# Two mixture-of-experts stages of a fused decoder: which engine does the elementwise work, and what TensorE does while the tokens are routed

## The chip, the cores and the metric

One core of one Trainium2 chip. The metric is the device time of one launch in microseconds, the median of three runs. The whole program is one kernel: twelve stages in a fixed order, each a block of instruction streams for the engines TensorE (PE), VectorE (DVE), ScalarE (ACT), GpSimd (POOL) and SyncE (SP), joined by semaphores. Between two stages all engines meet.

## The reference

The reference is a decoder with four layers; each has attention, cross attention and a feed-forward part, and after each `x = layernorm(x + part(x))`. x has 8 batches of 256 tokens, 256 wide, all float32. The change touches the feed-forward parts of layers 0 and 1:

```python
def _moe_forward(x, router_w, w1, w2, shared_gate_up, shared_down, shared_gate_w):   # layer 0: E = 8, K = 2, F = 256
    logits = xf @ router_w
    probs = softmax(logits)
    topw, topi = top_k(probs, K)
    combine = zeros((n, E)).at[arange(n)[:, None], topi].add(topw)
    h = silu(einsum('nd,edf->nef', xf, w1))
    ye = einsum('nef,efd->ned', h, w2)
    routed = einsum('ne,ned->nd', combine, ye)
    gu = xf @ shared_gate_up
    gate, up = (gu[:, :F], gu[:, F:])
    shared = silu(gate) * up @ shared_down
    shared = sigmoid(xf @ shared_gate_w) * shared
    return routed + shared

def _L1_ffn_ref(x, expert_sel, keys, values, route_scale):                           # layer 1: 16 experts of 64, K = 4
    sel_val, sel_index = the four largest of sigmoid(x @ expert_sel), divided by their sum, times route_scale
    scores_all = relu(einsum('btd,edh->bteh', x, keys))
    values_all = einsum('bteh,ehv->btev', scores_all, values)
    out = sum over the four chosen experts of sel_val * values_all
```

## The kernel before, in words

`moe_silu` (stage 2, from L2621) has three stretches.

The front. TensorE makes the logits of all 2048 tokens; VectorE takes the softmax and the two best experts of each, counts the tokens of each expert with two TensorE products (`counted`), and works out a place for each of the 4096 choices in 39 tiles of 128 rows, no tile with two experts. Four `at_place` products by VectorE and `to_table` on TensorE turn that into a table; `rows_known` says that the lists `holds` (which row a slot reads) and `dest` (where its result goes) are there. Meanwhile the shared expert is worked out for `EARLY` = 5 of the 8 batches: `sh_gate` and `sh_up` (8 matmul instructions each) on TensorE, Silu and a copy of the up half on ScalarE, their product on GpSimd (`sh_prod`, L3115), `sh_out` on TensorE, scaled on ScalarE, added to x_nat by GpSimd (`sh_add`, L3122). There is one buffer each of gate, up, product and scaled result.

The tiles. For tile t GpSimd issues an indirect DMA that gathers its rows into one of `XB` = 8 buffers (`gather`, L3127), and one that scatters the tile's result `ye` to the DRAM tensor `planes` (L3147): plane 0 for first choices, plane 1 for second. Its queue is 8 gathers, the add of batch 4, then gather t+8 and scatter t in turn. TensorE, in iteration i, transposes the rows of tile i (`rows_in`), multiplies tile i-1 by w1 (`hidden`), transposes tile i-2 (`hidden_turned`) and multiplies tile i-3 by w2 (`product`). ScalarE copies the turned rows out of the T bank and takes Silu out of the R bank; VectorE copies the turned hidden rows and `ye`, which has `YB` = 4 buffers. T, R and O banks alternate by t % 2.

The tail. When all scatters have landed SyncE reads the planes back in 8 DMAs (quarter q has batches 2q and 2q+1, both planes in one semaphore). TensorE, VectorE and ScalarE work out the shared expert for batches 5 to 7. `summed(q)` on VectorE, `weighed(q)` on ScalarE and `joined(q)` on GpSimd together form x + w0 plane0 + w1 plane1; VectorE takes the statistics, GpSimd the root (`root`), ScalarE normalises (`normed`), TensorE transposes and ScalarE copies to x_t (`turned`).

`moe_relu` (stage 5, from L3175) computes all 16 experts densely. A batch has four groups g of hidden rows (`hidden`, 8 matmul instructions, into one of four R banks), a `spread` that lays the token weights out over the hidden rows (4 matmuls into both T banks, copied to `gates` by ScalarE, twice a batch), `clipped` on VectorE (max with 0, times `gates`, from R to `hid`) and `outputs` (32 instructions). Iteration i of its loop does spread and hidden of batch i, outputs of i-1 and `transposed` of i-2. While VectorE routes, TensorE does the hidden groups of batch 0 and then 22 warming instructions (`keep_warm`, L212), whose results nobody reads.

## Time and profile before

| what | value |
|---|---|
| median of 3 runs | 3213.68 us (3212.23 to 3215.28) |
| the profiled execution | 3215.56 us, of it 3213.8 us span |
| mean granted TensorE clock | 0.97 |
| silu mixture | 988.6 to 1182.2 us |
| relu mixture, routing and loop | 1958.6 to about 2112 us |

"Idle before, releaser" says how long an engine stood idle before an instruction and what ended that; "issue" is time in which nothing that the profile shows was waited for. A granted clock of 1.0 is 2.4 GHz, 0.5 is 1.2 GHz. A fp32 matmul of the code is two instructions in the trace.

### The profile page before, as it was taken

The page shows a single profiled execution, that of the slowest core. Times are in us where ns is not written, and L with a number is a line of the kernel's source. Part 1 is how long each engine was busy: PE and PEld are TensorE (multiplying, and loading weights), DVE is VectorE, ACT ScalarE, POOL GpSimd, SP SyncE. Part 2 cuts the span into 40 slices and gives each one's busy share as a digit, 9 for nine tenths or more (in the row PEclk, how much of TensorE's full clock was granted, in tenths as well). Part 3 has the DMA queues.
Part 4 walks back from the last instruction along what each step waited for, and adds up shares of the span by engine and source line. Part 5 has one row for each costly group of instructions (what it writes and reads, how often), then busy time and mean ns, then how long its engine had stood idle before and what let it go on. Part 6 is the DMA issues. An engine that isn't in the chain of part 4 may idle for free. (4 is left out here: it accounts for less than half of the span.)

```text
span 3213.8 us, 55170 instructions
## 1 busy us (share of the span) xinstructions
PE 2937.8 (91%) x22706; PEld 1864.2 (58%) x22706; DVE 1674.5 (52%) x3021; ACT 1232.3 (38%) x2685; POOL 395.8 (12%) x602
## 2 busy tenths in 40 slices
PE   6999899999998968799999998989989899989898
PEld 3565556666655746556666656856656433336576
DVE  4666444444444344444444443324547799985532
ACT  1333255454442333145444441113323476643111
POOL 1111100000003720000000000000111100000222
PEclk9999999999999979899999999989999999999899
DMA  2001000000011331000000000010000100000242
GB/s 111 17 15 66 9 1 1 1 1 1 1 63 58 98 108 47 9 1 1 1 1 1 1 34 17 1 32 19 17 24 14 46 1 1 1 11 23 96 147 74
DMA packets 40623, 93.81 MB, mean 29 GB/s; under 512 B 4632, under 2 KB 32518, under 8 KB 36792
## 3 DMA queue, kind: packets, MB, share of 16 engines
q1 hardware_dynamic: 34583, 76.70, 6.8%
q0 software_dynamic: 5792, 13.59, 1.4%
q8 instruction: 183, 3.00, 0.4%
q14 instruction: 65, 0.52, 0.1%
HBM read 61.69 MB, written 14.03 MB: 24 GB/s over the span
## 5 line engine op out<-in xcount | busy, mean ns | idle before, releaser
L2337 ACT ACTIVATE prob<-R,neg_max 128x333 f32<-128x333 f32 x512 | 268.6, 538 | 182.4 <-DVE neg_max L2407 182.4
L3893 DVE TENSOR_TENSOR_SCAN arena<-arena,u 128x512 f32<-128x512 f32 x256 | 289.5, 1200 | 0.1
L2407 DVE TENSOR_REDUCE neg_max<-R 128x2 f32<-128x666 f32 x256 | 205.5, 844 | 97.1 <-PE R L2217 97.1
L2413 DVE COPY prob_t<-T 128x384 f32<-128x384 f32 x256 | 141.6, 553 | 188.6 <-PE T L2228 184.2
L2228 PEld LDWEIGHTS T<-const,prob 128*128 128x128 f32 (+1 forms) x1536 | 183.3, 143 | 96.3 <-issue 66.2
L2228 PE MATMUL T<-const,prob 128*128 128x128 f32 (+1 forms) x1536 | 210.0, 273 | 19.7 <-DVE prob_t L2413 19.5
L2344 ACT ACTIVATE prob_t<-T 128x384 f32<-128x384 f32 x256 | 126.1, 493 | 213.4 <-PE T L2228 206.7
L3824 ACT ACTIVATE arena<-delta,neg_a 128x510 f32<-128x510 f32 x256 | 175.6, 714 | 43.7 <-DVE arena L3893 42.9
L2177 PE MATMUL O<-arena,keys_in 128*128 128x512 f32 (+1 forms) x384 | 183.8, 603 | 5.0 <-ACT arena L2318 2.4
L2520 POOL COPY rec_rows<-rec 128x256 f32<-128x256 f32 x128 | 51.2, 400 | 1000.2 <-DVE rec L2418 1000.2
L2172 PE MATMUL O<-keys_in,arena 128*128 128x333 f32 x512 | 170.3, 458 | 1.2 <-DVE arena L2388 1.2
L3727 PE MATMUL R<-arena,diag 64*64 64x512 f32 x1024 | 135.8, 620 | 24.3 <-DVE arena L3893 24.2
L2166 PE MATMUL O<-keys_in,arena 128*128 128x256 f32 x512 | 124.5, 387 | 3.2 <-ACT keys_in L2312 2.4
L2424 DVE TENSOR_TENSOR attn_t<-O,arena 128x256 f32<-128x256 f32 x128 | 53.8, 420 | 131.4 <-ACT arena L2349 131.4
L2188 PE MATMUL O<-arena,attn_t 128*128 128x256 f32 x512 | 117.4, 382 | 1.0 <-DVE ysb L2390 1.0
L2172 PEld LDWEIGHTS O<-keys_in,arena 128*128 128x128 f32 x512 | 88.1, 190 | 40.9 <-DVE arena L2388 7.4
L944 DVE TENSOR_REDUCE neg_max<-R 128x8 f32<-128x2048 f32 (+1 forms) x24 | 55.0, 2292 | 100.0 <-PE R L721 100.0
L2166 PEld LDWEIGHTS O<-keys_in,arena 128*128 128x128 f32 x512 | 92.2, 189 | 22.0 <-ACT q_t L2315 4.2
L2188 PEld LDWEIGHTS O<-arena,attn_t 128*128 128x128 f32 x512 | 94.9, 190 | 15.7 <-DVE ysb L2390 1.8
L2337 ACT ACTIVATION_READ_ACCUMULATOR prob<-R,neg_max 128x1 f32 x512 | 103.9, 203 | 0.0
L2243 PE MATMUL O<-prob_t,v 128*64 128x256 f32 (+1 forms) x768 | 99.2, 394 | 1.3 <-DVE prob_t L2413 1.3
L2177 PEld LDWEIGHTS O<-arena,keys_in 128*128 128x128 f32 (+1 forms) x384 | 60.2, 176 | 69.4 <-issue 51.5
(579 smaller groups left out, 5510.8 us busy)
## 6 DMA issues: line engine op xcount, KB each, us to landing
w<-w_dram SPq DMA_DIRECT2D x16, 1024.0 KB, 6.9
arena<-pack_dram SPq DMA_DIRECT2D x2, 4100.0 KB, 15.0
q_pad<-q_pad SPq DMA_DIRECT2D x24, 224.0 KB, 2.7
arena<-pack_dram SPq DMA_DIRECT2D x4, 1284.0 KB, 6.2
arena<-pack_dram SPq DMA_DIRECT2D x1, 4896.0 KB, 15.1
slots_in<-x_nat SPq DMA_DIRECT2D x2, 2048.0 KB, 8.2
arena<-planes SPq DMA_DIRECT2D x8, 512.0 KB, 7.5
arena<-k_nat SPq DMA_DIRECT2D x16, 224.0 KB, 2.7
```

The lines of the kernel that those rows point to most:

```text
L2166: last = nc.tensor.matmul(bank[:, h * T:(h + 1) * T], wq[:, c, (2 * i + h) * P:(2 * i + h + 1) * P], keys[:, c, CTX:XK], start=(c == 0), s ...
L2172: last = nc.tensor.matmul(bank[:, 0:XK], wkv[:, c, i * P:(i + 1) * P], keys[:, c, :], start=(c == 0), stop=(c == C - 1))
L2177: last = nc.tensor.matmul(bank[0:n, :], keys[:, c, first:first + n], wkv[:, c, XI + i % 2 * BANK:XI + (i % 2 + 1) * BANK], start=(c == 0), ...
L2188: last = nc.tensor.matmul(bank[:, 0:D], attn_t[:, b % 2, c, i * P:(i + 1) * P], wo[:, c, :], start=(c == 0), stop=(c == HP - 1))
L2228: last = nc.tensor.transpose(S.T[0:n, i, kc * P:(kc + 1) * P], prob[:, g % 2, i, first:first + n], S.ident)
L2337: last = nc.scalar.activation(prob[:, g % 2, i, :], S.R[:, g % 2, i * BANK:i * BANK + XK], ACT.Exp, bias=neg_max[:, g % 2, i:i + 1], accum ...
L2344: nc.scalar.activation(prob_t[:, m % 2, 1, :, qt * P:(qt + 1) * P], S.T[:, 1, 0:3 * P].rearrange("p (c q) -> p c q", c=3), ACT.Copy).then_ ...
L2407: nc.vector.tensor_reduce(neg_max[:, g % 2, :], S.R[:, g % 2, :].rearrange("p (i n) -> p i n", i=2)[:, :, 0:XK], AX.X, ALU.max, negate=Tru ...
L2413: nc.vector.tensor_copy(prob_t[:, m % 2, 0, :, qt * P:(qt + 1) * P], S.T[:, 0, 0:3 * P].rearrange("p (c q) -> p c q", c=3)).then_inc(M.pt_ ...
L3727: last = nc.tensor.matmul(sums(i, a)[to:to + HB, :], diag[rows, i % CT, n + a, :], state[rows, (q + a) % HELD, :], start=(a == 1 and n == ...
L3824: nc.scalar.activation(decay[:, q % DEEP, :].rearrange("p (b t) -> p b t", b=PAIR)[:, :, 1:T], delta[:, i % 2, :].rearrange("p (b t) -> p ...
L3893: nc.vector.tensor_tensor_scan(state[:, q % HELD, :], decay[:, q % DEEP, :], u[:, i % 2, :], 0.0, ALU.mult, ALU.add)\
```

## The change

In the silu mixture GpSimd keeps the gathers, the scatters and the small root steps; `sh_prod`, `sh_add` and `joined` leave it. VectorE multiplies gate by up straight from the R bank and adds the scaled result; gate and product buffers are double; `scaled` and 16 `weight` matrices (the identity times each token's second weight, made by ScalarE in the tiles) lie in the unused end of the other weight image. On TensorE the counts come ahead of sh_out(0), sh_out(3) and sh_gate(4) stand ahead of the last two table groups, and the batches 5 and 6 of the shared expert are worked out between the tiles at fixed iterations; for that the tiles use one T and one R bank, and `ye` has 6 buffers. The expert numbers are worked out after `rows_known`. In the tail, TensorE sums x and the weighted second plane in eight PSUM banks (`residual`, `second_choices`), VectorE adds the weighted first plane in one step a token tile (`sums`), and turning starts by batch.

In the relu mixture nine groups (batches 0 and 1, and group 0 of batch 2) are multiplied during the routing, clipped into `hid` (three buffers now) by ScalarE, and weighted by VectorE in place once the gates are there; groups 1 to 3 of batch 2 follow the first spread, and the 22 warming instructions go. One DRAM tensor, `context_values`, is declared and not used.

```diff
-    XB, YB = 8, 4
+    XB, YB = 8, 6
...
+    GATE_AT, UP_AT, OUT_AT = {8: 5, 20: 6}, {11: 5, 23: 6}, {15: 5, 27: 6}
...
+    spare, used = S.arena[(k + 1) % 2], sum(n for _, n in PACK[k + 1].values())
+    scaled = spare[:, used:used + NT * D].rearrange("p (t d) -> p t d", t=NT)
+    weight = spare[:, used + NT * D:used + NT * (D + P)].rearrange("p (t n) -> p t n", t=NT)
...
+        sg = sb("sg", [P, 2, FC * T])
+        prod = sb("prod", [P, 2, FC * T])
...
+        banks = [S.O[:, 0, :], S.O[:, 1, :], S.R[:, 0, 0:BANK], S.R[:, 0, BANK:], S.T[:, 0, :], S.R[:, 1, 0:BANK], S.R[:, 1, BANK:], S.T[:, 1, :]]
         block = ctx.enter_context(nc.Block())
+
+        def shared_bank(b, up):
+            return S.R[:, b % 2 if b < EARLY else 1, up * BANK:(up + 1) * BANK]
 
...
+                    sp.dma_start(plane[:, j, 4 * q:4 * q + 4, :], rows.rearrange("(t p) d -> p t d", p=P))\
+                        .then_inc(second_in[q] if j else first_in[q], 16)
...
             sh_up(1)
-            sh_out(0)
             pe.wait_ge(G.picked, 1)
             pe.wait_ge(S.o_free[0], 1)
             flat = pick[:].rearrange("p j t e -> p (j t e)")
             nc.tensor.matmul(S.O[:, 0, 0:J * E], ones, flat, start=True, stop=True)
             nc.tensor.matmul(S.O[:, 1, 0:J * E], tri, flat, start=True, stop=True).then_inc(G.counted, 1)
-            sh_gate(2)
-            sh_up(2)
+            sh_out(0)
             sh_out(1)
-            sh_gate(3)
-            sh_up(3)
+            for b in (2, 3):
+                sh_gate(b)
+                sh_up(b)
             sh_out(2)
             to_table(0)
             to_table(1)
+            sh_out(3)
             sh_gate(4)
             to_table(2)
             to_table(3).then_inc(G.tabled, 1)
             sh_up(4)
-            sh_out(3)
             sh_out(4)
 
...
-                if t >= 2:
-                    pe.wait_ge(G.xt_sb, t - 1)
-                elif t == 1:
-                    pe.wait_ge(G.sh_scaled, EARLY)
+                if t >= 1:
+                    pe.wait_ge(G.xt_sb, t)
                 for c in range(C):
-                    last = nc.tensor.transpose(S.T[:, t % 2, c * P:(c + 1) * P], xe[:, t % XB, c * P:(c + 1) * P], S.ident)
+                    last = nc.tensor.transpose(S.T[:, 0, c * P:(c + 1) * P], xe[:, t % XB, c * P:(c + 1) * P], S.ident)
...
-                if t >= 2:
-                    pe.wait_ge(G.hid_sb, t - 1)
-                else:
-                    pe.wait_ge(G.sh_gate_sb if t == 0 else G.sh_up_sb, EARLY)
+                pe.wait_ge(G.hid_sb if t else G.sh_gate_sb, t or EARLY)
                 for c in range(C):
-                    last = nc.tensor.matmul(S.R[:, t % 2, 0:D], xe_t[:, t % 2, c, :], W[:, bass.ds(w + (w1_at + c * D), D)],
+                    last = nc.tensor.matmul(S.R[:, 0, 0:D], xe_t[:, t % 2, c, :], W[:, bass.ds(w + (w1_at + c * D), D)],
...
+                if i in GATE_AT:
+                    sh_gate(GATE_AT[i])
+                if i in UP_AT:
+                    sh_up(UP_AT[i])
+                if i in OUT_AT:
+                    sh_out(OUT_AT[i])
...
+            def residual(b):
+                pe.wait_ge(G.sh_added, b + 1)
+                nc.tensor.matmul(banks[b], S.ident, S.x_nat[:, b * TT:(b + 1) * TT, :].rearrange("p t d -> p (t d)"),
+                                 start=True, stop=False, skip_group_check=True)
+
+            def second_choices(q):
+                pe.wait_ge(second_in[q], 16)
+                for tt in range(4 * q, 4 * q + 4):
+                    last = nc.tensor.matmul(banks[tt // TT][:, tt % TT * D:(tt % TT + 1) * D], weight[:, tt, :], plane[:, 1, tt, :],
+                                            start=False, stop=True, skip_group_check=True)
+                last.then_inc(G.summed, 1)
...
+            def turned(b):
+                pe.wait_ge(G.normed, b + 1)
...
+            sh_gate(B - 1)
+            sh_up(B - 1)
+            pe.wait_ge(G.weights_made, NT)
+            for b in range(4):
+                residual(b)
+            sh_out(B - 1)
+            second_choices(0)
+            residual(4)
+            pe.wait_ge(G.sh_gate_sb, B)
+            residual(5)
+            second_choices(1)
+            residual(6)
+            second_choices(2)
+            turned(0)
+            turned(1)
+            residual(7)
+            second_choices(3)
+            for b in range(2, B):
+                turned(b)
...
+                if b >= 2:
+                    act.wait_ge(G.sh_prod, b - 1)
+                nc.scalar.activation(sg[:, b % 2, :], shared_bank(b, 0), ACT.Silu).then_inc(G.sh_gate_sb, 1)
...
-            for b in range(1, EARLY):
-                sh_gate(b)
...
-            sh_out(EARLY - 1)
+            sh_gate(1)
+            act.wait_ge(G.picked, 1)
+            sh_out(0)
+            sh_out(1)
+            sh_gate(2)
+            sh_gate(3)
+            sh_out(2)
+            sh_out(3)
+            sh_gate(4)
+            sh_out(4)
...
+                if i in GATE_AT:
+                    sh_gate(GATE_AT[i])
+                if i in OUT_AT:
+                    sh_out(OUT_AT[i])
+                if i < NT:
+                    nc.scalar.activation(weight[:, i, :], S.ident, ACT.Copy, scale=top[:, i, 1:2]).then_inc(G.weights_made, 1)
...
+            sh_gate(B - 1)
+            sh_out(B - 1)
...
+                    if tt % TT == TT - 1:
+                        last.then_inc(G.normed, 1)
...
+            def sh_prod(b):
+                dve.wait_ge(G.sh_gate_sb, b + 1)
+                dve.wait_ge(G.sh_up_full, b + 1)
+                if b >= 2:
+                    dve.wait_ge(G.sh_out_full, b - 1)
+                nc.vector.tensor_tensor(prod[:, b % 2, :], sg[:, b % 2, :], shared_bank(b, 1), ALU.mult).then_inc(G.sh_prod, 1)
+
+            def sh_add(b):
+                dve.wait_ge(G.sh_scaled, b + 1)
+                x = S.x_nat[:, b * TT:(b + 1) * TT, :]
+                nc.vector.tensor_tensor(x, x, scaled[:, b * TT:(b + 1) * TT, :], ALU.add).then_inc(G.sh_added, 1)
+
+            sh_prod(0)
+            sh_prod(1)
             dve.wait_ge(G.counted, 1)
             nc.vector.tensor_copy(count[:], S.O[:, 0, 0:J * E].rearrange("p (c e) -> p e c", c=J))
...
             for i in range(4):
+                if i % 2 == 0:
+                    sh_prod(2 + i // 2)
                 some = slice(i * J // 4, (i + 1) * J // 4)
...
             nc.vector.tensor_scalar(holds[:], second[:], -1.0, 0.0, ALU.add, ALU.max)
             dve.drain().then_inc(G.rows_known, 1)
+            sh_prod(4)
+            nc.vector.tensor_tensor(behind[:], steps[:, 0:NS].unsqueeze(2).to_broadcast([P, NS, E]),
...
+            nc.vector.tensor_copy(expert_at[:], expert_f[:])
+            dve.drain().then_inc(G.experts_known, 1)
+            dve.wait_ge(G.x_rows, 16)
...
+                if i + 2 in UP_AT:
+                    sh_prod(UP_AT[i + 2])
+                if 2 <= i < 2 + EARLY:
+                    sh_add(i - 2)
+                if i in OUT_AT:
+                    sh_add(OUT_AT[i])
...
-                dve.wait_ge(plane_in[q], 32)
-                for tt in (4 * q, 4 * q + 1):
-                    nc.vector.scalar_tensor_tensor(plane[:, 1, tt, :], plane[:, 1, tt, :], top[:, tt, 1:2], S.x_nat[:, tt, :], ALU.mult, ALU.add)
-                dve.wait_ge(G.joined, q + 1)
-                for tt in (4 * q + 2, 4 * q + 3):
-                    nc.vector.scalar_tensor_tensor(plane[:, 0, tt, :], plane[:, 0, tt, :], top[:, tt, 0:1], S.x_nat[:, tt, :], ALU.mult, ALU.add)
-                dve.drain()
-                for tt in (4 * q, 4 * q + 1):
-                    nc.vector.scalar_tensor_tensor(plane[:, 0, tt, :], plane[:, 0, tt, :], top[:, tt, 0:1], plane[:, 1, tt, :], ALU.mult, ALU.add)
+            def sums(q):
+                dve.wait_ge(first_in[q], 16)
+                dve.wait_ge(G.summed, q + 1)
+                for tt in range(4 * q, 4 * q + 4):
+                    nc.vector.scalar_tensor_tensor(plane[:, 0, tt, :], plane[:, 0, tt, :], top[:, tt, 0:1],
+                                                   banks[tt // TT][:, tt % TT * D:(tt % TT + 1) * D], ALU.mult, ALU.add)
                 dve.drain()
...
-            sh_prod(0)
-            sh_prod(1)
             pool.wait_ge(G.x_rows, 16)
-            sh_add(0)
-            for b in range(2, EARLY):
-                sh_prod(b)
-                sh_add(b - 1)
             pool.wait_ge(G.rows_known, 1)
             for t in range(XB):
                 gather(t)
-            sh_add(EARLY - 1)
...
-            joined(0)
-            joined(1)
-            root(0)
-            joined(2)
-            root(1)
-            joined(3)
-            root(2)
-            root(3)
+            for q in range(4):
+                root(q)
...
+    RAW = 2 * G + 1
...
+        hid = sb("hid", [P, 3, HC, T])
...
+                n = G * (b - 1) + g + 1
                 if b >= 1:
-                    pe.wait_ge(M.exp_done, G * (b - 1) + g + 1)
+                    pe.wait_ge(M.raw_sb if n <= RAW else M.exp_done, n)
...
-            for g in range(1, G):
-                hidden(0, g)
-            keep_warm(nc, S, S.T[:, 1, :], 11)
+            for n in range(1, RAW):
+                hidden(n // G, n % G)
...
-                        if i >= 1:
+                        if i >= 1 and G * i + g >= RAW and i != RAW // G:
...
+                if i == 0:
+                    for n in range(RAW, G * (RAW // G + 1)):
+                        hidden(n // G, n % G)
...
+            for n in range(RAW):
+                act.wait_ge(M.s_full, n + 1)
+                b, g = n // G, n % G
+                nc.scalar.activation(hid[:, b, 2 * g:2 * g + 2, :].rearrange("p c t -> p (c t)"), hidden_bank(g), ACT.Relu).then_inc(M.raw_sb, 1)
...
+                if G * b + g < RAW:
+                    dve.wait_ge(M.raw_sb, G * b + g + 1)
+                    dve.wait_ge(M.kg_ready, 2 * b + g // 2 + 1)
+                    nc.vector.tensor_tensor(some, some, gates[:, g // 2, g % 2, :], ALU.mult).then_inc(M.exp_done, 1)
+                    return
...
+                nc.vector.scalar_tensor_tensor(some, hidden_bank(g), 0.0, gates[:, g // 2, g % 2, :], ALU.max, ALU.mult).then_inc(M.exp_done, 1)
```

## Rows read from the trace of the kernel before

**Rows 1.** The page, part 1: busy time, share of span and instructions of each engine.
```profile
PE 2937.8 (91%) x22706; PEld 1864.2 (58%) x22706; DVE 1674.5 (52%) x3021; ACT 1232.3 (38%) x2685; POOL 395.8 (12%) x602
```

**Rows 2.** Timeline, GpSimd: start, duration, engine, line, operation, count [idle before, releaser].
```profile
1030.33 1.22 POOL L3128 DMA_INDIRECT xe<-slots_in,holds  x1 [0.18 <-issue]
...
1039.39 0.94 POOL L3128 DMA_INDIRECT xe<-slots_in,holds  x1 [0.30 <-issue]
...
1041.80 0.97 POOL L3128 DMA_INDIRECT xe<-slots_in,holds  x1 [0.17 <-issue]
...
1131.90 0.98 POOL L3147 DMA_INDIRECT planes<-ye,dest  x1 [0.30 <-issue]
```

**Rows 3.** Timeline, tiles 0, 6 and 7: first result copied, rows transposed.
```profile
1039.86 0.42 DVE L3061 COPY ye<-O 128x256 f32<-128x256 f32 x1 [0.44 <-PE O L2816]
...
1043.99 0.38 PE L2789 MATMUL T<-const,xe 128*128 128x128 f32 x2
...
1046.16 0.38 PE L2789 MATMUL T<-const,xe 128*128 128x128 f32 x2
```

**Rows 4.** Windows: stretch, us, busy by PE, PEld, DVE, ACT, POOL, clock, DMA share, GB/s.
```profile
1140.00:1184.00 44.00, 18.35 (x63) 14.09 (x62) 23.17 (x73) 16.46 (x33) 10.14 (x13) 0.64 0.20 63
```

**Rows 5.** Timeline, relu mixture: warming, first hidden groups of the loop, one round.
```profile
1967.93 9.60 PE L212 MATMUL T<-ctx_t,const 128*128 128x512 f32 x22
...
1985.24 5.39 PE L3226 MATMUL R<-x_t,arena 128*128 128x256 f32 x16
...
1994.66 7.07 PE L3245 MATMUL O<-arena,hid 128*128 128x256 f32 x32
...
2001.66 0.61 PE L3235 MATMUL T<-gate_t,expand 64*128 64x256 bf16 x4
...
2002.30 1.02 ACT L3310 ACTIVATE gates<-T 128x1024 f32<-128x1024 f32 x1 [10.07 <-PE T L3235]
...
2009.94 7.07 PE L3245 MATMUL O<-arena,hid 128*128 128x256 f32 x32
```

**Rows 6.** Timeline, front of the silu mixture, TensorE's block and VectorE's chain.
```profile
992.72 1.89 PE L2722 MATMUL R<-x_t,arena 128*128 128x256 f32 x8
...
1002.75 0.42 DVE L2987 COPY count<-O 128x256 f32<-128x256 f32 x1 [2.55 <-PE O L2766]
...
1003.24 1.82 DVE L2989 TENSOR_TENSOR_SCAN until<-carry,count 128x256 f32<-128x256 f32 x1
...
1013.51 2.52 DVE L3021 TENSOR_TENSOR at_value<-at_tile,order 128x1248 bf16<-128x1248 bf16 x1
...
1024.00 0.24 DVE L3037 COPY table<-O 128x78 f32<-128x78 f32 x1
...
1025.45 0.18 DVE L3046 TENSOR_SCALAR holds<-second 128x39 uint32<-128x39 f32 x1
```

**Rows 7.** Timeline, tail: the product of gate and up on VectorE.
```profile
1134.44 0.69 DVE L3068 TENSOR_TENSOR prod<-sg,R 128x512 f32<-128x512 f32 x1 [4.04 <-PE R L2722]
```

**Rows 8.** Line L3025: durations in ns min/median/max, first and last start, shapes.
```profile
L3025 DVE TENSOR_TENSOR at_place<-const,place x4: 1225/1226/2281, 1016.0 to 1021.0; 128x1024 bf16<-128x1024 f32 x4
```

**Rows 9.** The page, part 5: the scans of another stage, busy, mean ns.
```profile
L3893 DVE TENSOR_TENSOR_SCAN arena<-arena,u 128x512 f32<-128x512 f32 x256 | 289.5, 1200 | 0.1
```

**Rows 10.** Timeline, around tile 6: copies out of the T bank and the R bank.
```profile
1044.41 0.38 ACT L2901 ACTIVATE xe_t<-T 128x256 f32<-128x256 f32 x1 [0.92 <-PE T L2789]
...
1045.50 0.42 DVE L3054 COPY hid_t<-R 128x256 f32<-128x256 f32 x1 [0.88 <-PE R L2808]
```

**Rows 11.** Timeline, tail: first sum, the last quarter's sums and statistics, last copy.
```profile
1139.76 0.88 DVE L3081 SCALAR_TENSOR_TENSOR arena<-arena,top,x_nat 128x256 f32<-128x256 f32 x2 [4.63 <-DMA arena<-planes]
...
1171.64 0.87 DVE L3084 SCALAR_TENSOR_TENSOR arena<-arena,top,x_nat 128x256 f32<-128x256 f32 x2
...
1175.55 0.16 DVE L3096 TENSOR_SCALAR mv<-mv 128x4 f32<-128x4 f32 x1
...
1181.63 0.60 ACT L2927 ACTIVATE x_t<-O 128x512 f32<-128x512 f32 x1 [0.25 <-PE O L2854]
```

165 lines of the change are left out of this document (41 added, 124 removed).

## The prediction

> **What bounds the kernel now.** I read the page first: TensorE is busy for 91% of a span of 3213.8 us, GpSimd (POOL) for 12% [rows 1]. That average hides the two stages that are edited, so I read those by the timeline and a table by window.
>
> The silu mixture runs from 988.6 to 1182.2 us and has three stretches. In the front, routing decides which rows each of 39 tiles holds. In the tiles, GpSimd issues one gather and one scatter per tile. Both stand on one queue: each is about 1 us long, and ahead of each lie some 0.30 us of "issue" [rows 2]. From 1041.80 to the end of the last scatter (1132.9) that queue never rests: 91.1 us for 70 instructions (31 gathers, 39 scatters), 1.30 each, 2.60 a tile [rows 2]. TensorE, where rows are already fetched, takes a tile every 2.17 us (1043.99 to 1046.16, [rows 3]), so GpSimd ends last and TensorE has 0.43 us a tile to spare. The tail, from 1132.9, is a chain of VectorE, GpSimd and ScalarE steps; TensorE is busy 18.35 of 44 us there at a mean granted clock of 0.64 [rows 4].
>
> The relu mixture is TensorE alone: from outputs to outputs (32 matmuls, 7.07 us) it runs through, with 8.28 us of spread and hidden products between (2001.66 to 2009.94) [rows 5]. While VectorE routes, TensorE burns 22 warming matmuls for 9.60 us [rows 5]: time in which nothing is computed.
>
> **Part A, the front: when the first gather starts.** Now rows_known comes at about 1025.7 (holds, 1025.45 + 0.18 [rows 6]), but the first gather starts at 1030.33 [rows 2]: GpSimd still has prod(4), issued when TensorE's sh_out(3) frees the buffer, and x_nat(3) in its queue. The change takes both away: 4.6 us.
>
> rows_known itself moves too. VectorE now sits idle 2.55 us, from 1000.20 to 1002.75, for the counts [rows 6], since sh_out(0) stands ahead of them on TensorE; after the change the counts come first (about 1001.6) and sh_prod(0), sh_prod(1) (0.69 each, [rows 7]) fill the wait: the chain starts again at about 1001.8, 0.95 us earlier. Two-input VectorE work is also stretched while GpSimd computes: of four equal at_place products one took 2281 ns, the others 1226 [rows 8]; the scan over 256 took 1.82 and at_value 2.52 [rows 6], against about 0.6 and 1.5 at the rates of their unstretched like (the 512-wide scan of 1200 ns halved, [rows 9]; 1226 ns for 1024 columns scaled to 1248). With no GpSimd arithmetic these three give 1.2 + 1.0 + 1.05 = 3.2 us. Added are sh_prod(2) and (3), 1.4 us. So VectorE has its last at_place at 1022.3 - 0.95 - 3.2 + 1.4 = 1019.5.
>
> The page "SBUF — State Buffer" of the Trainium skill, section "Who interferes with whom", says that a VectorE instruction with two SBUF inputs contends with a GpSimd instruction that reads SBUF, and that one waits for the other; the at_place rows agree (one of four doubled).
>
> But TensorE now ends this part last. Its queue from the counts (1001.6): eight 1.89 us blocks of eight matmuls (as at 992.72, [rows 6]; sh_out(0), sh_out(1), gate and up of 2 and 3, sh_out(2), sh_out(3)) and sh_gate(4), nine in all, 17.0 us; about 1.0 and 0.3 us, an estimate from two 256-wide ScalarE copies like those of [rows 10], in which sh_out(1) and sh_out(3) wait for the T bank; four table groups, 1.4 (32 bf16 matmuls of 78 columns at the rate of the spread's four of 256, 0.61 us [rows 5]). Sum 19.7: the table is full at 1021.3, where now it is copied at 1024.00 [rows 6]. Gain 2.7. VectorE's 1019.5 is earlier, so this stands. I take 7.0 for A (4.6 + 2.7, less 0.3 for wake-ups). Bounds: 8.5 if VectorE's end decides, 3.5 if TensorE loses its clock there as it does now. The later "behind" chain and sh_prod(4) (2.4 us) are hidden by the first gather's flight, about 3 us.
>
> **Part B, the tiles.** x_nat(4) leaves the GpSimd queue between gathers 7 and 8: the ninth, now at 1041.80, follows at 1039.39 + 0.94 + 0.30 = 1040.63, 1.2 us earlier [rows 2]. The 70 instructions behind stay as they are, 91.1 us. Into the same stretch go, on TensorE, six blocks of 1.89 us (11.3 us); on ScalarE 16 weight planes (about 0.27 each), two Silus and two scaled copies; on VectorE seven adds and two products. I cost them at nothing, with this cover: the first ye is written at 1039.86 + 0.42, 9.95 us after the first gather [rows 2, 3]; without x_nat(4) its scatter is due at 11.6, and tile t is due at 11.6 + 2.60 t while TensorE delivers at 9.95 + 2.17 t plus the blocks already run. At tiles 6, 9, 13, 18, 21 and 25 the margin is 2.3, 1.7, 1.6, 1.8, 1.2 and 1.0 us: thin, but never below zero, and six ye buffers in place of four let VectorE write ahead (it waits on the scatters now). If the cover went, each us short is a us lost, at most the last block and a half, 3 us. ScalarE idles 0.92 us ahead of each xe_t copy and VectorE 0.88 us ahead of each hid_t copy [rows 10]: a weight plane or a 0.69 us add fits.
>
> **Part C, the tail.** Now the last scatter starts at 1131.90 and the last x_t copy ends at 1182.23: 50.3 us [rows 2, 11]. After it, on the same clock less 8.2 (A + B): TensorE is free at 1122.5; gate and up of batch 7 to 1126.2; four residual products, each two matmuls of 0.436 (22 took 9.60, [rows 5]), 3.5, to 1129.7; sh_out(7) 1131.6; second_choices(0), again eight matmuls of 256 columns, 1133.5. The first planes have landed by then (now used at 1139.76, 7.9 us after the last scatter starts [rows 2, 11]: 1131.6). VectorE then needs 4.2 us a quarter: from the second pair of sums to the end of the statistics, which holds four sums as a quarter does after the change, is 1171.64 to 1175.71 = 4.07 [rows 11], and a drain. The first pair of sums and the wait for GpSimd's join are gone. Four quarters: 1150.3. TensorE stays ahead: quarters 1, 2 and 3 are summed at 1137.1, 1139.8 and 1144.8, while VectorE asks at 1137.7, 1141.9 and 1146.1. Then what now follows the last statistics: 1175.71 to 1182.23 = 6.5 us [rows 11], less 0.8 since turning starts by batch and not by quarter. End: about 1156. That is 26.3 before 1182.2: part C is 26.3 - 8.2 = 18.1. Bounds: 19 (planes awaited, no TensorE wait), and 13 if TensorE runs at 0.50 after its first pause, as the mean of 0.64 makes likely for part of it [rows 4], which adds about 3 to the quarter 3 sum and 2 elsewhere.
>
> **Part D, the relu rows.** Five more hidden groups (8 matmuls, 1.86) are done in place of the 9.60 us of warming: 9.3 us, which ends where setup ends now, so the start does not move; nine Relu copies of 0.6 run on an idle ScalarE. In the loop, iteration 2 has only two spreads, with ScalarE's gate copy of 1.02 us bare between them: about 2.3 us where 8.28 stood, 6.0 gained [rows 5]. In iterations 0 and 1, the hidden products of batch 1 (1985.24 to 1994.66; the first 16 of its matmuls took 5.39 us, against 3.8 for two blocks of [rows 6]) give way to three groups and one more bare gate copy: outputs(0) at about 1992.9 in place of 1994.66, 1.8 gained [rows 5]. Together 7.8. Bounds 5.5 (clock low throughout) and 9.3 (all of the work taken out, no new wait).
>
> **The sum.** 7.0 + 1.2 + 18.1 + 7.8 = 34.1 us. The profiled execution took 3215.56 us (span 3213.8, 1.8 around it): 3181.5. The median of the runs is 1.9 lower than the profiled one; taken off the median 3213.68, it is 3179.6, and I say 3180.
>
> **The rivals.**
> 1. *VectorE's adds hold up GpSimd's DMA issue.* Seven adds and two products of 0.69 us fall in the tiles; if GpSimd stood still for each, 6.2 us: 3186. For it: the doubled at_place row [rows 8]. Against: a gather took 0.94 before VectorE's copies began and 0.97 beside them [rows 2, 3]. The same section of the Trainium skill infers that descriptor generation needs the write interface, which a tensor_tensor leaves alone; by that the price is 0, and only a run can show it here.
> 2. *TensorE a little late in the tiles.* The margins of 1 to 2 us are eaten (one bank of T and of R each, where two alternated) and GpSimd starves: 3 to 6 us, 3184.
> 3. *The single banks decide (slower than before).* Each tile now reuses one T and one R bank, so TensorE must wait until ScalarE has read xe_t (0.38) and hid (about as long) and VectorE hid_t (0.42), some 0.1 each to wake [rows 10]. If these 1.5 us came bare in each tile, a tile would be 2.17 + 0.29 + 1.5 = 3.96 against 2.60: 39 x 1.36 = 53 lost, 34 gained: 3233. It turns the sign from 1.0 us bare a tile. Against: xe_t is read by 1044.79 and its bank is wanted again at 1046.16 [rows 3, 10].
> 4. *The clock.* TensorE stays at 0.5 in tail and relu entry: C and D at their low bounds less a part, 5 us: 3185.
> 5. *The front gives less:* TensorE's queue is late or at half clock: 3.5 for 7.0: 3183.5.
> 6. *The relu rows bring nothing,* the routing end moving with the last Relu: 3188.
>
> **Chances.** Forecast 0.52; rivals 1 to 6: 0.12, 0.12, 0.03, 0.10, 0.08, 0.03. Range 3173 to 3190: all but the slower case and pairs of misses above, a few unstretched operations that I have not counted below. About 0.2% (6.4 us) is what a measurement of this kernel can tell: faster 0.96, same 0.01, slower 0.03.
>
> **What would show it.** The gap from holds to the first gather falls from 4.7 to under 0.5 us; gathers and scatters stay at 1.30 each with no wait on ye (rivals 1 to 3 show as longer instructions, or waits on VectorE's ye); TensorE never waits on xe_t, hid or hid_t; the last scatter to the last x_t copy is about 32 us; four equal steps of 4.2 us on VectorE in the tail; the warming row is gone from the relu mixture and outputs(0) to outputs(1) is about 9.4 us. The prediction is wrong if the 2.60 us a tile changes, or if the tail waits for planes.

## The result: 14 to 26 us faster, where 34 were forecast

The changed kernel took 3201.11 us (median of 7 runs, 3180.41 to 3206.06) beside 3215.28 us before (7 runs, 3207.55 to 3226.67): ratio 0.9945 with a 95% interval of 0.9928 to 0.9961. Repeated in three more groups of runs, on two chips, the same pair of kernels gave 0.9952 [0.9937, 0.9967], 0.9925 [0.9910, 0.9941] and 0.9927 [0.9905, 0.9948]. The sign was right. The forecast of 3180 us is reached by the fastest execution alone, which happens to be the profiled one, and the median lies outside the range.

| | before | after |
|---|---|---|
| median | 3215.28 us | 3201.11 us |
| profiled execution, its span | 3215.56, 3213.8 us | 3180.41, 3178.6 us |
| granted TensorE clock, mean | 0.970 | 0.975 |
| silu mixture | 193.7 us | 175.0 us |
| of it: front, tiles, tail | 41.8, 101.6, 50.3 | 34.2, 102.6, 38.3 |
| end of the perceiver and relu mixture | 223.6 us | 213.2 us |

The stretches are cut by rows of the timelines. The silu mixture begins with SyncE's write of slots_in, its front ends with the first gather, its tiles with the start of the last scatter, its tail with the last x_t copy. The relu stretch (the table's last row, which takes in the end of the perceiver, the stage ahead of the relu mixture) goes from SyncE's prefetch of the next weights to the last rows normalised on VectorE. SyncE's rows of the changed kernel, then of the kernel before:

```profile
984.26 0.39 SPq L2697 DMA_DIRECT2D slots_in<-x_nat  x1
1860.11 72.75 SPq L193 DMA_DIRECT2D arena<-pack_dram  x2
```

```profile
988.55 0.39 SPq L2691 DMA_DIRECT2D slots_in<-x_nat  x1
1884.20 74.71 SPq L193 DMA_DIRECT2D arena<-pack_dram  x2
```

GpSimd, changed kernel, end of the tiles and tail (it answers to [rows 2]):

```profile
1116.50 0.98 POOL L3147 DMA_INDIRECT planes<-ye,dest  x1 [0.61 <-issue]
1118.44 0.98 POOL L3147 DMA_INDIRECT planes<-ye,dest  x1 [0.96 <-DVE ye L3098]
1119.73 0.98 POOL L3147 DMA_INDIRECT planes<-ye,dest  x1 [0.30 <-DVE ye L3098]
1121.02 0.98 POOL L3147 DMA_INDIRECT planes<-ye,dest  x1 [0.30 <-issue]
1134.70 1.03 POOL L3154 TENSOR_TENSOR rstd<-mv,const 128x4 f32<-128x4 f32 x1 [12.70 <-DVEq L3122]
1142.27 0.20 POOL L3156 TENSOR_TENSOR shift<-mv,rstd 128x4 f32<-128x4 f32 x1 [6.54 <-issue]
1142.42 1.01 POOL L3154 TENSOR_TENSOR rstd<-mv,const 128x4 f32<-128x4 f32 x1
1143.57 0.20 POOL L3156 TENSOR_TENSOR shift<-mv,rstd 128x4 f32<-128x4 f32 x1
```

The scatters run at 1.29 us each, but near the end they wait for ye. Behind the first rstd (1134.70 to 1135.73) GpSimd stands for 6.54 us, with nothing to wait for but its own drain (`pool.drain()`, the one statement between rstd and shift). VectorE and ScalarE show what follows from that; in each timeline the number in brackets is the idle time ahead of the row:

```profile
1130.68 1.66 DVE L3111 SCALAR_TENSOR_TENSOR arena<-arena,top,O 128x256 f32<-128x256 f32 x4 [0.25 <-PE O L2852]
1134.77 1.65 DVE L3111 SCALAR_TENSOR_TENSOR arena<-arena,top,R 128x256 f32<-128x256 f32 x4 [0.19 <-issue]
1138.86 0.87 DVE L3111 SCALAR_TENSOR_TENSOR arena<-arena,top,T 128x256 f32<-128x256 f32 x2 [0.19 <-issue]
...
1149.69 0.87 DVE L3111 SCALAR_TENSOR_TENSOR arena<-arena,top,R 128x256 f32<-128x256 f32 x2 [6.93 <-PE T L2852]
...
1153.74 0.17 DVE L3121 TENSOR_SCALAR mv<-mv 128x4 f32<-128x4 f32 x1 [0.22 <-issue]
```

```profile
1142.51 2.07 ACT L2945 ACTIVATE x_nat<-arena,shift,rstd 128x256 f32<-128x256 f32 x4 [12.80 <-POOL shift L3156]
...
1158.68 0.60 ACT L2951 ACTIVATE x_t<-T 128x512 f32<-128x512 f32 x1 [0.38 <-PE T L2860]
```

The first three quarters go in steps of 4.09 us, as forecast (4.2). Then VectorE waits 6.93 us for TensorE. In TensorE's queue the last second-choice products stand behind the transposes of the first two blocks, these wait for the first normalised rows, and these for GpSimd's shift. TensorE's rows, the transposes first, then the last of the products that VectorE waits for:

```profile
1143.65 2.10 PE L2860 MATMUL O<-const,x_nat 128*128 128x128 f32 x8 [6.63 <-ACT x_nat L2945]
...
1148.55 1.03 PE L2852 MATMUL T<-arena 128*128 128x256 f32 x4
```

The tiles and the stage behind the mixture, by window (stretch, its length, busy us of PE, PEld, DVE, ACT and POOL, granted clock, DMA share, GB/s): before, then after.

```profile
1030.33:1131.90 101.57, 92.32 (x478) 74.36 (x477) 32.92 (x78) 30.79 (x80) 77.84 (x78) 0.98 0.31 93
1182.23:1343.65 161.42, 129.08 (x3624) 96.99 (x3624) 80.49 (x133) 45.23 (x73) 8.81 (x17) 0.87 0.16 53
```

```profile
1018.42:1121.02 102.60, 99.25 (x529) 84.14 (x530) 40.05 (x91) 37.35 (x102) 78.10 (x78) 1.00 0.30 92
1159.28:1317.89 158.61, 127.51 (x3624) 96.29 (x3624) 80.55 (x133) 45.29 (x73) 8.80 (x17) 0.87 0.16 53
```

TensorE is busy for 99.25 us of 102.60 in the tiles, where it was for 92.32 of 101.57: GpSimd is no longer alone at its limit.

### The profile page after: what moved, and what is told of

It reads as the page before. It is cut to its first block and busy times, and to the rows that moved or that the text cites. A ratio compares the mean times of both kernels' runs of the same rounds, so it can differ in the third digit from the quotient of the medians.

```text
span 3178.6 us, 55219 instructions
## 1 busy us (share of the span) xinstructions
PE 2924.4 (92%) x22732; PEld 1859.8 (59%) x22732; DVE 1670.7 (53%) x3020; ACT 1235.6 (39%) x2703; POOL 378.5 (12%) x588
## 5 line engine op out<-in xcount | busy, mean ns | idle before, releaser
L2344 ACT ACTIVATE prob_t<-T 128x384 f32<-128x384 f32 x256 | 125.9, 492 | 213.7 <-PE T L2228 206.9
L3826 ACT ACTIVATE arena<-delta,neg_a 128x510 f32<-128x510 f32 x256 | 174.3, 713 | 39.8 <-DVE arena L3895 38.6
L2172 PE MATMUL O<-keys_in,arena 128*128 128x333 f32 x512 | 170.2, 458 | 1.2 <-DVE arena L2388 1.2
L2337 ACT ACTIVATION_READ_ACCUMULATOR prob<-R,neg_max 128x1 f32 x512 | 103.7, 203 | 0.0
```

What stands on the lines that cost most here:

```text
L2172: last = nc.tensor.matmul(bank[:, 0:XK], wkv[:, c, i * P:(i + 1) * P], keys[:, c, :], start=(c == 0), stop=(c == C - 1))
L2337: last = nc.scalar.activation(prob[:, g % 2, i, :], S.R[:, g % 2, i * BANK:i * BANK + XK], ACT.Exp, bias=neg_max[:, g % 2, i:i + 1], accum ...
L2344: nc.scalar.activation(prob_t[:, m % 2, 1, :, qt * P:(qt + 1) * P], S.T[:, 1, 0:3 * P].rearrange("p (c q) -> p c q", c=3), ACT.Copy).then_ ...
L3826: nc.scalar.activation(decay[:, q % DEEP, :].rearrange("p (b t) -> p b t", b=PAIR)[:, :, 1:T], delta[:, i % 2, :].rearrange("p (b t) -> p ...
```

## All profiles by stretch

The same cuts for the runs below, in us; block 16 is the untouched stage behind the silu mixture, from the mixture's last x_t copy to its own.

| profile | silu mixture | front, tiles, tail | block 16 (clock) | relu stretch |
|---|---|---|---|---|
| before | 193.7 | 41.8, 101.6, 50.3 | 161.4 (0.87) | 223.6 |
| same_before | 193.8 | 43.2, 101.5, 49.1 | 158.5 (0.87) | 222.1 |
| same_before_2 | 193.9 | 41.6, 102.0, 50.3 | 159.1 (0.84) | 222.3 |
| relu_only | 193.7 | 43.2, 101.3, 49.3 | 158.5 (0.87) | 213.5 |
| before_busy_2 | 200.1 | 41.7, 107.4, 51.0 | 159.8 (0.85) | 222.1 |
| after | 175.0 | 34.2, 102.6, 38.3 | 158.6 (0.87) | 213.2 |
| same_after | 175.5 | 34.2, 102.7, 38.6 | 169.5 (0.82) | 213.2 |
| same_after_2 | 175.1 | 34.2, 102.6, 38.3 | 169.2 (0.84) | 213.2 |
| same_after_3 | 177.0 | 35.9, 102.6, 38.6 | 169.3 (0.82) | 213.2 |
| silu_only | 175.1 | 34.2, 102.6, 38.4 | 166.3 (0.84) | 223.5 |
| early_drain | 168.4 | 34.2, 102.7, 31.5 | 164.7 (0.84) | 213.2 |
| early_drain_2 | 170.2 | 35.9, 102.8, 31.5 | 165.6 (0.85) | 213.2 |
| tail_order | 173.6 | 34.2, 102.7, 36.7 | 166.9 (0.82) | 213.2 |
| drain_front | 168.9 | 32.4, 104.9, 31.5 | 167.9 (0.82) | 213.2 |
| no_adds | 177.0 | 35.9, 102.9, 38.2 | 164.7 (0.87) | 213.1 |
| long_tail_2 | 186.0 | 34.2, 102.8, 49.1 | 167.2 (0.83) | 213.2 |
| rest_behind | 187.9 | 35.9, 102.6, 49.5 | 167.5 (0.83) | 213.2 |
| on the chip with stalls: | | | | |
| before_busy | 215.5 | 42.2, 123.2, 50.0 | 165.0 (0.83) | 222.7 |
| long_tail | 209.8 | 34.2, 125.6, 50.0 | 168.9 (0.85) | 213.2 |
| relu_warm | 197.6 | 35.9, 123.7, 38.1 | 168.7 (0.85) | 219.9 |

## Experiments

**The kernel again, unaltered, and its halves.** same_after is the changed kernel; silu_only has the old relu mixture, relu_only the old silu mixture. early_drain adds one line on GpSimd ahead of the end of the tiles:

```
+            pool.drain()
             pool.sem_inc(G.past_tiles, 1)
```

> The changed kernel once more, unaltered, to see which of its executions is the typical one: its first seven lie between 3180 and 3206 us. Theory A (the edits are worth what the first trace of after shows, some 27 us in the two edited stages; the rest is the clock of TensorE in stages that no edit touches): most executions near 3200, a ratio to the kernel before of 0.993 to 0.996, and in the new trace the silu mixture again 175 us long (first logits to last x_t copy) and the relu mixture again 8 us shorter than before, with any further difference from the first trace outside the two. Theory B (the edits give back part of their gain in most executions, through TensorE's clock in the tiles, whose first trace was a lucky one): the silu mixture 185 us or more in a trace of a 3200 us execution, with the granted clock below 1 between 1025 and 1120 us.

> The silu part of the change alone; moe_relu is that of before. If the parts simply add, as the first trace says: 18.5 us less than before in the silu mixture, and the following entry 1.5 us; the time 8 us above the changed kernel. If theory B holds for the silu part, its ratio to before is that of the changed kernel (0.995), or nearer to 1.

> The relu part alone; moe_silu is that of before. The first trace of after has it at 8.0 us from relu start to the next stage's weights; then ratio 0.9975 to before. If the warming products that it takes away kept the clock up for what follows, the gain is under 4 us and the granted clock of the loop's first 10 us lower than in the kernel before.

> One drain more on GpSimd, right behind its last scatter, where it then idles 12.7 us for the first statistics. In the trace of after the first root waits 6.54 us between rstd and shift (the same 6.54 us stood in the trace before); the later three wait 0.2 us. Theory C (the first drain behind the indirect DMAs costs this once, wherever it stands): the new drain takes it off the path, shift(0) follows rstd(0) by 0.1 us, turned(0) no longer holds up second_choices(3), VectorE's wait of 6.93 us ahead of the last sums goes and the silu mixture is 6 to 7 us shorter than in the changed kernel: 168 to 169 us. Rival D (it is the first use of the product, or code that is fetched, and not the drain): the gap stays 6.5 us and the time does not move.

Measured on one chip, before at 3218.92 us (17 runs, 3212.91 to 3226.01): same_after 3205.09, ratio 0.9952 [0.9937, 0.9967]; silu_only 3205.84, 0.9968 [0.9946, 0.9989]; relu_only 3199.94, 0.9947 [0.9929, 0.9965]; early_drain 3188.38, 0.9911 [0.9894, 0.9929].

By their stretches the two edits give 18.6 us (193.7 to 175.1) and 8.6 to 10.4 us (222.1 to 223.6 against 213.2 to 213.5), the same in every profile of these kernels but for the 1.7 us by which the front comes late in some. By the medians the halves gain 13.1 and 19.0 us and the whole 13.8: they don't add, and neither half came where it was expected. silu_only lies 0.75 us above the changed kernel and not 8; relu_only has 0.9947 and not 0.9975, more than its stretch is worth. What is between stretches and medians lies outside the edits. The span of the changed kernel was 3178.6 us in one profile and 3205.2 in another, and the silu mixture has 0.5 us of these 26.6. By SyncE's prefetches 8.2 lie in the first stage, ahead of both edits (297.6 to 305.8 us), 9.0 in block 16 and the perceiver, and 11.0 in cross16, far behind (124.5 to 135.5; the kernel before had 125.9 to 133.3). Theory B falls: the tiles were as long in the slower profile, 102.7 us.

early_drain settled the 6.54 us. GpSimd in its tail:

```profile
1124.99 0.99 POOL L3147 DMA_INDIRECT planes<-ye,dest  x1 [0.30 <-issue]
1138.67 1.04 POOL L3155 TENSOR_TENSOR rstd<-mv,const 128x4 f32<-128x4 f32 x1 [12.69 <-DVEq L3122]
1139.85 0.20 POOL L3157 TENSOR_TENSOR shift<-mv,rstd 128x4 f32<-128x4 f32 x1
```

The shift follows the rstd by 1.18 us in place of 7.57, and the tail takes 31.5 us, which is what the prediction had (32). So theory C stands and rival D falls: the first drain behind the indirect DMAs costs these 6.54 us, once, and ahead of the statistics, where GpSimd waits 12.69 us anyway, it costs nothing (how long it takes there, no row shows). It was in the kernel before too, where I had not asked for it. There GpSimd's additions of the tail (`joined`) stand between the last scatter and the first root and show no such gap:

```profile
1149.83 1.03 POOL L3160 TENSOR_TENSOR rstd<-mv,const 128x4 f32<-128x4 f32 x1
1157.40 0.21 POOL L3162 TENSOR_TENSOR shift<-mv,rstd 128x4 f32<-128x4 f32 x1 [6.54 <-issue]
```

**How much of the tail is the queue's order?** tail_order leaves the drain late and moves two transposes:

```
             second_choices(2)
-            turned(0)
-            turned(1)
             residual(7)
             second_choices(3)
-            for b in range(2, B):
+            for b in range(B):
```

> The changed kernel with one edit in TensorE's queue: the transposes of the first two blocks stand behind the last second-choice products instead of ahead of them; the late first root stays as it is. Theory F (in the tail the late first root costs twice, once by its own 5 us and once because the transposes that wait for it hold the last products and with them VectorE's last sums, 6.93 us): last sums wait under 1 us, from the last scatter to the last copy 32 to 34 us instead of 38.3, silu mixture 169 to 171 us instead of 175, 4 to 6 us off the median. Theory G (only the root's own lateness counts, the order does not): 175 us again, since the copies of the first two blocks now come late instead, median as the changed kernel within 3 us.

Ratio 0.9929 [0.9910, 0.9948], 3195.54 against 3216.93 us. VectorE's 6.93 us are gone (0.19), yet the tail takes 36.7 us: 1.6 less than 38.3, not 4 to 6. Theory F had the mechanism of the wait and the wrong price. ScalarE is next late; from its first normalised rows to its last copy it takes 3.8 us a quarter, 3.3 of them busy:

```profile
1144.56 2.07 ACT L2943 ACTIVATE x_nat<-arena,shift,rstd 128x256 f32<-128x256 f32 x4 [12.79 <-POOL shift L3154]
...
1148.34 2.06 ACT L2943 ACTIVATE x_nat<-arena,shift,rstd 128x256 f32<-128x256 f32 x4
...
1159.12 0.60 ACT L2949 ACTIVATE x_t<-T 128x512 f32<-128x512 f32 x1 [0.38 <-PE T L2860]
```

So what starts ScalarE late is mostly paid at the end: against early_drain it starts 6.4 us later behind the last scatter, and the tail is 5.1 us longer. The order of the transposes is a detail behind it.

**Front and tiles.** drain_front is early_drain with the table's last two parts ahead of the shared expert's fourth output and fifth gate; no_adds leaves five of the seven additions out:

```
+            to_table(2)
+            to_table(3).then_inc(G.tabled, 1)
             sh_out(3)
             sh_gate(4)
-            to_table(2)
-            to_table(3).then_inc(G.tabled, 1)
```

```
             def sh_add(b):
                 dve.wait_ge(G.sh_scaled, b + 1)
+                if b < EARLY:
+                    dve.sem_inc(G.sh_added, 1)
+                    return
```

> The drain of GpSimd put ahead of the end of the tiles as in early_drain, and in the front of the silu mixture all four parts of the row table ahead of the fourth output and fifth gate of the shared expert in TensorE's queue. If these two stand in the way of the table (it waits 2.39 us for TensorE in the changed kernel), the first gather comes 1 to 2.5 us earlier (32 to 33 us behind the start of the mixture instead of 34.2) and the mixture takes 166 to 167.5 us instead of 168.4. If VectorE's one-hot planes set the table's time, 168.4 us again. Either way nothing else moves, and the median is that of early_drain (3188 us) less 0 to 2 us, which this many rounds can hardly tell from nothing.

> The changed kernel without the five additions of the first five blocks' shared expert to x_nat on VectorE during the tiles; they are left out, so the output lacks that term. Rival 1 of the prediction (VectorE's additions hold GpSimd's indirect DMAs): no indirect DMA of the tiles takes longer than about 1.0 us, where the changed kernel has five of 1.4 to 1.5, and first gather to last scatter takes 100 to 101 us instead of 102.6. Otherwise 102.6 us again and the stretched ones stay where they are.

In drain_front (3190.93 us; no_adds had 3192.1 in a single execution) the first gather comes 1.8 us earlier, as TensorE's queue was indeed what the table waited for, and the tiles take 2.2 us longer: the shared blocks moved behind the table now stand ahead of the first tile, and GpSimd waits 2.99 us for ye at 1035.13. The mixture gains nothing (168.9 against 168.4, expected 166 to 167.5), nor does the median (0.9914 [0.9895, 0.9933]).

In the changed kernel a few gathers and scatters are stretched beside VectorE's additions:

```profile
1031.63 1.46 POOL L3135 DMA_INDIRECT xe<-slots_in,holds  x1 [0.31 <-PE T L2792]
1036.00 1.47 POOL L3147 DMA_INDIRECT planes<-ye,dest  x1 [0.31 <-issue]
1040.37 1.39 POOL L3135 DMA_INDIRECT xe<-slots_in,holds  x1 [0.30 <-DVE ye L3098]
```

Each began within 0.15 us of an addition (1031.56, 1035.89 and 1040.23); two additions that fell inside a running instruction, and the two later ones, stretched nothing. Without the additions none of these three is above 1.02 us, so the cause that rival 1 named is real, at 0.4 to 0.5 us for three of the seven additions. (The first gather is long in either kernel, 1.48 and 1.47 us.) But the tiles take 102.9 us all the same, not the 100 to 101 expected: what GpSimd saves it then waits for ye, at the end of the tiles:

```profile
1119.46 0.98 POOL L3150 DMA_INDIRECT planes<-ye,dest  x1 [1.04 <-DVE ye L3101]
1121.63 0.98 POOL L3150 DMA_INDIRECT planes<-ye,dest  x1 [1.19 <-DVE ye L3101]
1123.57 0.98 POOL L3150 DMA_INDIRECT planes<-ye,dest  x1 [0.96 <-DVE ye L3101]
```

In the changed kernel TensorE and GpSimd end together, and what GpSimd alone gains, in the front or in the tiles, it waits for ye. A gain on TensorE alone was not run.

**What happens in block 16?** With the old mixture ahead of it this stage takes 158.5 to 161.4 us in four profiles, with the new one 164.7 us or more in all but one. The first test is a fuller TensorE in the old tiles, the second two long rests of TensorE in the new tail, both on top of early_drain:

```
-                for c in range(C):
-                    last = nc.tensor.matmul(S.R[:, t % 2, 0:D], ...
+                for _ in range(1 + t % 2):
+                    for c in range(C):
+                        last = nc.tensor.matmul(S.R[:, t % 2, 0:D], ...
```

```
+            act.wait_ge(G.rstd_ready, 1)
+            for _ in range(16):
+                nc.scalar.activation(sg[:], sg[:], ACT.Copy)
+                act.drain()
             normed(0)
```

This is long_tail; in rest_behind the copies wait for `G.xt_new` instead and stand ahead of `turned(B - 1)`.

> The kernel before, unaltered, for a second profile of it. Two profiles of the changed kernel (3178.6 and 3205.2 us of span) differ by 26.6 us, almost all of it outside the two edited mixtures, with TensorE's granted clock (0.975 and 0.971). Theory A (this spread belongs to the untouched stages and to either kernel): the silu mixture takes 193 to 194 us again and the end of the perceiver with the relu mixture 238 us again, while the untouched stages differ by several us from the first profile (block 16 and the perceiver 689 us there, cross16 in stage 7 125.9 us). Theory E (the new silu mixture leaves the chip in a state that slows the stages behind it): block 16 and the perceiver stay at or under 690 us, while the three profiles of the new mixture with a late clock had 695 to 699 us.

> The kernel before, with the hidden products of every second tile of the silu mixture computed twice in place (19 times 0.87 us, 16.5 us more of TensorE in the tiles, which is about as full as the changed kernel has it; same output). In three profiles with the old silu mixture the stage behind it (block 16, from the mixture's last copy to its own) took 158.1, 158.5 and 161.4 us at a mean granted clock of 0.87; in seven with the new one 158.6 to 169.5 us, six of them 164.7 or more, clock 0.82 to 0.87. Theory H (TensorE without gaps in the tiles is what lowers the clock of the stage behind): block 16 takes 164 to 170 us at 0.82 to 0.84, and the median rises by 6 us or more beyond what the tiles themselves gain in length. Theory I (it is the shorter, emptier tail, or something else): 158 to 161.5 us at 0.87 again.

> early_drain with sixteen copies of 128x1024 of a finished buffer onto itself on ScalarE ahead of the first normalised rows, so that TensorE rests some 17 us longer in the tail of the silu mixture (same output). The mixture takes 184 to 188 us instead of 168.4. Theory I (the shorter tail gives TensorE less rest, and the stage behind pays for it by the clock): block 16 takes 158 to 161 us at 0.87 instead of 164.7 at 0.84. Theory H (the full tiles): 164 to 170 us at 0.82 to 0.84 again.

> The kernel before once more, for a profile beside the other three. Theory H (TensorE's full tiles lower the clock of the stage behind): block 16 takes 158 to 161.5 us at 0.87. If instead it is the chip that differs, 164 us or more at 0.83 or 0.84. If this chip stalls ScalarE and VectorE as the one before did, the tiles (first gather to last scatter) take more than the 101.5 us of the two earlier profiles; without stalls 101.5.

> The kernel before with 16.5 us more of TensorE work in the tiles of the silu mixture. Theory H: block 16 164 to 169 us at 0.82 to 0.85, that is 4 us or more above same_before_2. If block 16 is within 2 us of same_before_2, theory H falls. The tiles themselves 0 to 3 us longer where nothing stalls, 10 us or more where ScalarE and VectorE stall.

> early_drain with sixteen copies on ScalarE between TensorE's last transposes and the last copy to x_t, so that TensorE rests some 18 us directly ahead of block 16 (same output). Mixture 168.4 us plus 18 to 20. Theory L (a rest ahead of block 16 is what gives it the better clock): block 16 takes 158 to 162 us with a mean granted clock of 0.87. Theory M (the rest has nothing to do with it): 164 to 170 us at 0.82 to 0.85, as same_after_3.

> The long tail once more, its rest of TensorE ahead of the first normalised rows. Theory L in its weaker form (any rest in the tail counts): block 16 158 to 162 us. Theory M: 164 to 170 us. Without the stalls of the other chip the tiles take 102.7 us and the mixture 186 to 188 us.

> The changed kernel as the control on this chip: mixture 175 us, block 16 164 to 170 us (in one of three profiles it was 158.6).

same_before: 3217.09 us (same_before_2 3213.61), and the stretches of the kernel before again; block 16 and the perceiver together took 686.5 us (1190.71 to 1877.23 between SyncE's prefetches), so theory E's sign is borne out (686.1 to 689.2 in all five profiles with the old mixture, 689.7 to 700.2 in the twelve with the new one), though not the state of the chip that it speaks of. before_busy: 3239.63 against 3232.32, 1.0023 [1.0010, 1.0037]; before_busy_2: 3225.06 against 3217.64, 1.0018 [1.0004, 1.0031]. The first had 165.0 us in block 16 and seemed to bear out theory H; it ran on the chip with the stalls, without a kernel before beside it. On one chip with its control it has 159.8 against 159.1 us, with TensorE busy 103.40 us of 107.41 in the tiles, 96%, as full as the changed kernel's (99.25 of 102.60, 97%). Theory H falls, by this one profile. before_busy_2, tiles and block 16:

```profile
1029.13:1136.54 107.41, 103.40 (x553) 88.27 (x552) 33.03 (x78) 30.77 (x80) 77.95 (x78) 1.00 0.29 88
1187.50:1347.30 159.80, 131.20 (x3624) 99.26 (x3624) 80.50 (x133) 45.36 (x74) 8.83 (x17) 0.85 0.16 53
```

A rest doesn't help either: 18 us of it inside the tail gave 167.2 us (long_tail_2) and directly ahead of block 16 167.5 us (rest_behind), beside 169.3 in same_after_3. Theories I and L fall and M stands, one profile each. Their medians were 3213.0 and 3213.65 us against 3219.89. The same 3624 matmuls, in same_after:

```profile
1168.04:1337.50 169.46, 135.80 (x3624) 102.29 (x3624) 80.70 (x133) 45.35 (x73) 8.84 (x17) 0.82 0.15 50
```

Against the block of the first changed profile TensorE is busy 8.29 us more (135.80 less 127.51) of the 10.85 us by which it is longer, at 0.82 instead of 0.87. But the clock isn't all of it. same_before_2 and silu_only have the same granted clock and the same busy time on TensorE in this block, and still lie 7.2 us apart, all of it idle time of TensorE (26.03 and 33.25 us):

```profile
1182.72:1341.80 159.08, 133.05 (x3624) 99.19 (x3624) 80.51 (x133) 45.24 (x73) 8.84 (x17) 0.84 0.17 53
1163.97:1330.25 166.28, 133.03 (x3624) 99.64 (x3624) 80.71 (x133) 45.29 (x74) 8.81 (x17) 0.84 0.16 51
```

So what is shown is that block 16 is longer behind the new mixture. By what, clock, waits or both, is not found; the place of the kernel's new buffers and its longer code were not varied.

**The chip with the stalls.** The three profiles of one chip have tiles of 123 to 126 us. relu_warm there, at 1062.85 and 1064.34, where VectorE and ScalarE stand idle for 2 us each, with no releaser that fits:

```profile
1062.85 0.42 DVE L3091 COPY hid_t<-R 128x256 f32<-128x256 f32 x1 [2.05 <-remote]
1064.34 0.38 ACT L2924 ACTIVATE xe_t<-T 128x256 f32<-128x256 f32 x1 [2.25 <-DMA q_pad<-neg_t]
1065.53 1.01 POOL L3147 DMA_INDIRECT planes<-ye,dest  x1 [2.36 <-DVE ye L3098]
```

> The changed kernel once more. On a chip without the stalls: tiles 102.6 us, silu mixture 175 us, block 16 164 to 170 us, median 13 to 16 us under the kernel before. On one with the stalls: tiles up to 124 us, since TensorE has no gap left in which to make up for them, and the median within 6 us of the kernel before.

> The changed kernel with GpSimd's first drain put at the end of the tiles, once more: 6 to 7 us less in the mixture than same_after_2 on any chip (the drain doesn't hang on stalls or clock), median 6 to 17 us under same_after_2, 20 to 30 us under the kernel before without stalls, 5 to 12 us with them.

That it goes with the chip, and not with a kernel, is shown by long_tail, 125.6 us there and 102.8 on another, and in the busy old tiles, 123.2 and 107.4 (this chip was used in one group of runs only). I had thought that the changed kernel, with its full TensorE, would lose its advantage there. The medians don't show that: against the kernel before on the same chip long_tail had 0.9992 [0.9977, 1.0006] there and 0.9983 [0.9962, 1.0004] elsewhere. The next four ran where nothing stalls, before at 3217.64 us: same_after_2 3195.82, 0.9925 [0.9910, 0.9941], 21.8 us under the kernel before where 13 to 16 were expected; early_drain_2 3188.62, 0.9902 [0.9888, 0.9916]. What stalls the two engines stays open, and so does whether the old tiles, which have gaps, would absorb it.

**The warming matmuls.** relu_warm puts one line back ahead of the gates:

```
+            keep_warm(nc, S, S.T[:, 1, :], 11)
             settle(pe, M.setup, 1)
```

> The changed kernel with the eleven warming matmuls of the old relu mixture put back ahead of the gates. Causal16, the untouched stage behind the relu mixture, took 244.4 to 246.6 us in three profiles with the old relu mixture (clock 0.74 in its first 21 us) and 239.8 to 242.6 us in seven with the new one (0.92 and 0.84 there). Theory J (the warming matmuls cost that clock): 244 to 247 us again, and the relu mixture itself no longer than 1 us more. Theory K (the warming doesn't matter; what counts is that the 13.98 us of hidden products stand earlier): 240 to 243 us.

3226.97 us against 3232.32, 0.9990 [0.9970, 1.0010]. The relu stretch takes 219.9 us instead of 213.2. I expected at most 1 us, and missed that the hidden products now fill the time in which the warming was free. TensorE without it (changed kernel) and with it:

```profile
1936.70 13.98 PE L3216 MATMUL R<-x_t,arena 128*128 128x256 f32 x64
1951.56 1.03 PE L3258 MATMUL T<-const,gate_wide 128*64 128x128 f32 x8 [0.88 <-PEq L218]
...
1956.62 7.13 PE L3216 MATMUL R<-x_t,arena 128*128 128x256 f32 x24
...
1965.95 7.17 PE L3235 MATMUL O<-arena,hid 128*128 128x256 f32 x32
```

```profile
1972.46 13.98 PE L3216 MATMUL R<-x_t,arena 128*128 128x256 f32 x64
1986.28 9.60 PE L212 MATMUL T<-ctx_t,const 128*128 128x512 f32 x22
1995.71 1.04 PE L3259 MATMUL T<-const,gate_wide 128*64 128x128 f32 x8
...
2000.78 5.45 PE L3216 MATMUL R<-x_t,arena 128*128 128x256 f32 x24
```

The gates start 8.4 us later on TensorE (23.25 us behind the first hidden products against 14.86), and 24 matmuls run in 5.45 us instead of 7.13, at a granted clock of 1.00 instead of 0.76: the clock that the warming holds up gives back 1.7. The stage behind, causal16, took 240.0 us between SyncE's prefetches, as theory K had it. But same_before_2, with the old relu mixture, then had 238.6, so the stage's length does not tell the two mixtures apart as J and K took for granted.

## Why the prediction was right and wrong

**Part A, right.** First gather at 34.16 us behind the start of the mixture against 41.78: 7.6 us, forecast 7.0 (34.2 to 35.9 against 41.6 to 43.2 in all profiles that leave the front as it is). Its two terms miss in opposite directions: the lists are ready 3.8 us earlier, forecast 2.7, and the gap behind them shrinks by 3.8, forecast 4.3. The upper bound of 8.5 does not come out of its own terms: VectorE's 1019.5 against 1022.3 and 4.6 make 7.4. The unstretched operations came as worked out, and TensorE's queue, not VectorE, ended the part (what answers to [rows 6]):

```profile
1005.56 1.45 DVE L3053 TENSOR_TENSOR at_value<-at_tile,order 128x1248 bf16<-128x1248 bf16 x1
1007.53 2.56 DVE L3059 TENSOR_TENSOR at_place<-const,place 128x1024 bf16<-128x1024 f32 x2
1015.86 0.24 DVE L3063 COPY table<-O 128x78 f32<-128x78 f32 x1 [2.39 <-PE O L2757]
1017.33 0.18 DVE L3072 TENSOR_SCALAR holds<-second 128x39 uint32<-128x39 f32 x1
```

at_value 1.45 for 2.52, and the four at_place 1.22 to 1.23 each with none doubled. From holds to the first gather there are still 0.91 us, not under 0.5.

**Part B, wrong by 2.2 us.** 102.6 us from first gather to last scatter where 100.4 were due. The step that failed is "I cost them at nothing". The margins were taken tile by tile against GpSimd's 2.60 us, up to tile 25. Over the last eight tiles, where no gathers are left, GpSimd asks for a tile every 1.30 us and TensorE delivers every 2.17, so the end depends on how far ahead TensorE is, and 11.3 us of shared expert had taken that away. Carried on to tile 38, the prediction's own terms give an estimate of 9.95 + 38 x 2.17 + 11.3 = 103.7 us for TensorE, where the scatter is due at 11.6 + 30 x 2.60 + 8 x 1.30 = 100.0. In the rows of the changed kernel the 2.2 us appear as 1.5 us of longer instructions on GpSimd (rival 1: three of them beside additions, and the first gather) and 0.6 us more of waiting for ye (rival 2). Which of the two is the limit, no_adds told: with the additions gone the waits took their place. So this is rival 2 at a smaller price than its 3 to 6 us, and rival 1 is real but hidden behind it. Rival 3 falls: TensorE waited on its single banks twice in the tiles, 0.5 us in all, at the first tiles.

**Part C, wrong by 6.0 us.** 12.1 us gained (50.3 to 38.3) for 18.1. Planes, the start of the sums and the first three quarters of VectorE came as written, and so did what follows the last statistics: 5.4 us, from the end of the row at 1153.74 to 1159.28, forecast 6.5 less 0.8. The step that failed is "TensorE stays ahead", with quarter 3 summed at 1144.8 for VectorE's 1146.1. It gave the transposes ahead of those products their busy time and no wait for the first normalised rows. Measured, TensorE waits 6.63 us there, the products end at 1149.58, and VectorE, which asks at 1142.76, waits 6.93 us. Behind it stands a term put at nothing: GpSimd's first drain behind the indirect DMAs (6.54 us) had stood beside a longer chain in the tail of before; [rows 11] don't show it, and I did not read GpSimd's rows between its last scatter and its last root. With the drain moved, the tail has the length that I forecast (31.5 for 32); with the transposes moved instead, it does not (36.7), so the drain is the cause and the queue's order a way in which it acts.

**Part D, right, at its upper bound.** 213.2 us against 222.1 to 223.6: 9 to 10 us, forecast 7.8 and its bound 9.3. outputs(0) to outputs(1) takes 9.36 us, forecast 9.4. The size was missed at the entry of the loop: 24 hidden matmuls take 7.13 us there, and outputs(0) comes 33.4 us behind the first products of the stage (1932.58 to 1965.95), 2.7 us sooner than before (1958.63 to 1994.66), forecast 1.8.

**The rest: a stage that no edit touches.** The parts as measured are 18.2 + 9.5 = 27.7 us (means of the profiles of the unaltered old and new mixtures on chips without stalls). Block 16 takes 159.5 us behind the old mixture (mean of five profiles on chips without stalls) and 166.5 behind the new one (mean of twelve): 7.0 us are given back, which leaves 21. Against this the four groups of runs have 14.2, 13.8, 21.8 and 26.0 us between their medians, mean 19.0. That is within 2 us of the sum, but no proof of it: the groups differ by more, and so do stages that the sum leaves out (causal16 243.9 us in the mean behind the old relu mixture and 241.3 behind the new one, cross16 124.5 to 135.5, the first stage 297.6 to 305.8). The step that failed is one that the prediction does not write down: it had every other stage at nothing. Rival 4 had the clock as a cause, at 5 us, in the tail and the relu entry. The entry does show it (7.13 us for 24 matmuls at 0.76, against 5.45), and Part D came out all the same; whether the clock is what lengthens block 16 stays open. The forecast for the median was made from a single execution's stretches, as if all that lies outside them stood still; it does not, by 26.6 us between two profiles of one kernel.

**Best version.** early_drain, 0.9911 [0.9894, 0.9929] and 0.9902 [0.9888, 0.9916] of the kernel before, ahead of the changed kernel on both chips (3188.38 against 3205.09, 3188.62 against 3195.82).

## What to carry to other kernels

When a change shortens a chain, read every engine's rows through the whole stretch, not those of the old chain alone: an engine that stood behind the chain (here GpSimd's drain of 6.54 us) becomes late as soon as the chain is gone. Work laid beside a bound engine has to be costed to the end of the stretch, where the bound engine runs out of half of its work: margins that held for tile 25 were gone by tile 38. And where the untouched stages move by more than the edit, sum the edit by its stretches, in several profiles, and give the median a range of its own.

## What the runs showed of the hardware

- The first drain of GpSimd behind 78 indirect DMAs takes 6.54 us, to the hundredth in all profiles of both kernels, of the halves, tail_order, no_adds, relu_warm and the busy ones; between a later rstd and its shift lie 0.14. Laid into a wait of 12.69 us it costs nothing. Why it takes so long was not varied: neither the number of the DMAs nor their kind.
- An indirect DMA's instruction on GpSimd of 0.97 to 1.02 us took 1.39 to 1.47 where it began within 0.15 us of a two-input addition on VectorE (128x512, three of seven additions), and is back at its length without them.
- With GpSimd's arithmetic gone from the front, VectorE's products of 2.28 and 2.52 us ran in at most 1.23 and in 1.45.
- On one chip ScalarE and VectorE stood idle together about every 13 us in the tiles, for 2 us and more, with no releaser; the tiles were 16 and 23 us longer than the same kernels' elsewhere, and the medians 12 to 17 us (before 3232.32 us, elsewhere 3215.28 to 3219.89).
- Block 16, untouched, took 159.5 us behind the old silu mixture (five profiles) and 166.5 behind the new one (twelve). Two of these profiles have the same granted clock (0.84) and the same busy time on TensorE, and differ by 7.2 us.
